# A graph layer with routed experts: ScalarE compares tile numbers behind every fourth slot, 16-bit tables

## The chip, the cores and the metric

The kernel runs on one core of one Trainium2 chip. A core has five engines with queues of their own: PE (TensorE, the matmuls), DVE (VectorE), ACT (ScalarE), POOL (GpSimd) and SP (SyncE, which here only issues DMAs). They run side by side and meet through semaphores. The metric is the device time of one execution in microseconds; what is given is the median of some runs.

## What is computed

There are 3125 nodes with 256 features and 50,000 edges, sorted by destination. The destinations are drawn so that low nodes have most edges.

```python
def gnn(x, W1, b1, W2, b2, src, tgt):            # x is layer-normed
    feat = concat([x[tgt], x[src] - x[tgt]])
    h = relu(feat @ W1 + b1)                     # W1 512x512
    msg = h @ W2 + b2                            # W2 512x256
    out = segment_sum(msg, tgt)
    return out / (degree(tgt) + 1e-8)
def ffn(x):                                      # x is layer-normed
    logits = xn @ Wr + br                        # 8 experts, the best 2, softmax weights
    return sum over both: w * (gelu(xn @ W1[e] + b1[e]) @ W2[e] + b2[e])
x = x + gnn(layernorm(x), ...)
x = x + ffn(layernorm(x))
```

## The kernel before

The nodes lie in 25 tiles of 128 rows. An edge's hidden row is relu(p[dst] + q[src]), with q = x @ W1[lower half] + b1 and p = x @ (upper half less lower half). The sum over a tile's edges is taken before W2. The work has four stages with a barrier of all engines between them.

**Stage A (0 to 66 us).** Tile by tile the rows are normalised, turned, and multiplied to q, which goes to memory (q_rows). VectorE has in between the small work of the tables: from counts it finds where each tile's edges begin (`find_ends`, start_f), how many slots of 128 edges each has (last_f, nslot), the slot's first edge (`find_tiles`, `find_blocks`) and the tile of each slot (ttab). `unsorted` is a flag: where it is set, for edges out of order or tiles that come too soon, `n_pass` becomes 25 instead of 1 and the edges are gone over 25 times. That is the general path. With the reference's inputs the flag is 0. tile4_i holds the tile of each slot as integers, and DMAs copy it to tile_row (on one partition) and to tile_of_slot.

**Stage B, the edge loop (66 to 596 us).** It goes over 408 slots, written out one by one; a few steps called "half" between them make p for later tiles. For a slot j:
- POOL gathers its 128 rows of q into one of 16 places of gath (`fetch`, L1001). It may do so once the place was read, 16 slots back.
- ScalarE copies these rows into one of 5 PSUM banks (`seed`, L1231), or, for one slot in eight, VectorE adds them (`add_z`, L1063).
- PE adds p of the destination: a matmul with a one-hot matrix ohT, high and low part (`expand`, L1381 to L1385).
- ScalarE takes the relu into h_hi (`relu_hi`, L1250), VectorE the rest into h_lo (`split_lo`, L1068).
- PE sums the edges by destination into agg_ps (`sum_edges`, L1428 and L1429). agg_ps has two halves, used in turn by even and odd tiles.
- ScalarE closes the tile when the next slot has another one (`close`, L1252): it waits until PE has summed the slot, compares two registers with the tile numbers of this slot and the next, and if they differ copies the half out (L1260), fills it with zeroes (L1267) and waits for each. Otherwise it jumps over this.

Each engine's order is written out by its own function `first` with a lead: at a step ScalarE does the relu of 5 steps ahead, then the seed of 8 steps ahead, then the close of the slot itself. The relu of a slot waits for the sum four slots back (HI_RING). ScalarE loads the tile numbers of 17 slots into registers at every 16th slot (`load_tiles`, L952), PE four at every fourth.

**Stage C (596 to 685 us)** multiplies by W2, adds, normalises and sorts the tokens by expert. **Stage D (685 to 903 us)** goes over 56 expert slots: gather, two products, and a scatter with addition by POOL, whose waits come from a table turn_i.

## Time and profile before

| what | value |
|---|---|
| median of 3 runs | 1121.46 us (1121.32, 1121.46, 1126.88) |
| span of the profiled execution | 902.9 us |
| around the span, to the median | 218.6 us |
| PE, DVE, ACT, POOL busy | 834.7, 651.0, 628.3, 602.4 us |
| granted TensorE clock, mean | 0.995 |

The page gives the span from the first to the last instruction of the profiled execution, and no other time of it; the time of a run is longer. Register, branch, semaphore and DMA-issuing instructions are not counted as busy. A busy PE is not PE at its peak, since matmuls overlap.

### The profile page before, as it was taken

To read this page: it belongs to the slowest core of one execution; us is meant where nothing else is said; L and a number is where in the kernel's file an instruction comes from. 1 tells how busy PE (TensorE), PEld (TensorE's weight loads), DVE (VectorE), ACT (ScalarE), POOL (GpSimd) and SP (SyncE) were. 2 spreads that over 40 slices of the span, in tenths; PEclk is the share of its full clock that TensorE was granted. 3 is DMA by queue.
4 is the path that set the end of the run, shared out by engine and by line. 5 is a ranking of instruction groups with operands and counts; after the bars stand their busy time and mean duration, and the time that the engine had idled before them with its cause. 6 is when DMAs were issued, how large, how long until landed. Compare 5 with 4: busy or idle time off the path is not lost. (4 is left out here: it accounts for less than half of the span.)

```text
span 902.9 us, 17755 instructions
## 1 busy us (share of the span) xinstructions
PE 834.7 (92%) x4088; PEld 652.2 (72%) x4089; DVE 651.0 (72%) x1764; ACT 628.3 (70%) x1393; POOL 602.4 (67%) x615
## 2 busy tenths in 40 slices
PE   6997999999999989989999999989999999999997
PEld 3444767767676666766666666768888999999996
DVE  6846888888888888878888887756894455455443
ACT  4425788888888888888898889845554555555553
POOL 2317777777777777777777777659404677776764
PEclk9998999999999999999999999999999999999999
DMA  8547777878888778888887878819852344444443
GB/s 255 171 150 220 247 239 245 247 234 251 240 243 236 247 231 243 241 238 238 245 248 235 230 233 264 228 49 281 265 139 54 59 73 75 81 71 68 76 71 45
DMA packets 91000, 169.47 MB, mean 188 GB/s; under 512 B 17604, under 2 KB 56910, under 8 KB 90840
## 3 DMA queue, kind: packets, MB, share of 16 engines
q0 software_dynamic: 43696, 122.35, 49.8%
q1 hardware_dynamic: 46232, 44.79, 17.0%
q10 hardware_dynamic: 944, 0.92, 0.4%
q8 instruction: 44, 0.72, 0.3%
q14 instruction: 84, 0.69, 0.3%
HBM read 146.98 MB, written 21.43 MB: 187 GB/s over the span
## 5 line engine op out<-in xcount | busy, mean ns | idle before, releaser
L1001 POOL DMA_INDIRECT gath<-q_rows,idx_t x408 | 391.9, 960 | 138.8 <-issue 93.3
L1068 DVE SCALAR_TENSOR_TENSOR h_lo<-bank,h_hi 128x512 fp32r<-128x512 f32 x327 | 219.4, 682 | 40.1 <-ACT h_hi L1250 38.0
L1250 ACT ACTIVATE h_hi<-bank 128x512 fp32r<-128x512 f32 x327 | 191.0, 598 | 45.5 <-DVE bank L1063 20.9
L1231 ACT ACTIVATE bank<-gath 128x512 f32<-128x512 f32 x287 | 173.4, 604 | 14.3 <-DMA gath<-q_rows,idx_t 10.5
L1384 PE MATMUL bank<-p_hi,ohT 128*128 x287 | 123.4, 430 | 42.8 <-ACT bank L1231 40.3
L1428 PE MATMUL agg_ps<-h_hi,oh 128*128 128x512 f32 x408 | 161.9, 397 | 0.3 <-DVE h_lo L1068 0.2
L1429 PE MATMUL agg_ps<-h_lo,oh 128*128 128x512 f32 x408 | 161.3, 395 | 0.0
L1995 POOL DMA_INDIRECT out<-y_out,sca_i x56 | 93.7, 1673 | 49.0 <-issue 15.9
L1384 PEld LDWEIGHTS bank<-p_hi,ohT 128*128 128x128 f32 x287 | 54.1, 189 | 91.2 <-issue 83.0
L1385 PE MATMUL bank<-p_lo,ohT 128*128 x287 | 113.9, 397 | 0.0
L2099 PE MATMUL bank<-tokT,fw_now 128*128 128x128 f32 x896 | 109.3, 275 | 0.8 <-ACT tokT L2055 0.8
L2065 ACT ACTIVATE actT<-bank,b1T 128x128 f32<-128x128 f32 x224 | 64.0, 367 | 61.8 <-PE bank L2099 61.8
L2111 PE MATMUL agg_ps<-fw,actT 128*128 x448 | 105.9, 380 | 0.1
L2099 PEld LDWEIGHTS bank<-tokT,fw_now 128*128 128x128 f32 x896 | 104.5, 192 | 1.0 <-DVE fw_now L2018 1.0
L1428 PEld LDWEIGHTS agg_ps<-h_hi,oh 128*128 128x128 f32 x408 | 76.8, 188 | 27.4 <-issue 2.1
L1577 POOL DMA_INDIRECT agg_all<-xm_rows,gat_i x56 | 57.9, 1034 | 57.9 <-DVEq L1817 40.6
L1046 DVE TENSOR_SCALAR oh<-iota_row,rel_t 128x128 fp32r<-128x128 f32 x408 | 91.7, 296 | 4.7 <-issue 4.7
L2038 DVE TENSOR_TENSOR y_out<-agg_ps,b2f 128x256 f32<-128x256 f32 x56 | 23.8, 424 | 95.6 <-PE agg_ps L2111 87.6
L2111 PEld LDWEIGHTS agg_ps<-fw,actT 128*128 128x128 f32 x448 | 80.9, 190 | 9.0 <-issue 0.3
L1429 PEld LDWEIGHTS agg_ps<-h_lo,oh 128*128 128x128 f32 x408 | 76.9, 188 | 11.9
L1056 DVE TENSOR_SCALAR ohT<-rows_sb,slot_no 128x512 fp32r<-128x512 bf16 x102 | 52.1, 512 | 33.7 <-PE bank L1385 26.6
L2055 ACT ACTIVATE tokT<-bank,gain_T 128x128 f32<-128x128 f32 x112 | 45.0, 453 | 38.9 <-PE bank L2089 38.2
(287 smaller groups left out, 1276.6 us busy)
## 6 DMA issues: line engine op xcount, KB each, us to landing
rows_sb<-rel_blocks SPq DMA_DIRECT2D x102, 128.0 KB, 4.3
fw<-in_L_ffn_W SPq DMA_DIRECT2D x16, 512.0 KB, 5.1
gath<-q_rows,idx_t POOLq DMA_INDIRECT x408, 4.4
q_rows<-q_buf SPq DMA_DIRECT2D x25, 256.0 KB, 2.4
out<-x_all SPq DMA_DIRECT2D x28, 128.0 KB, 3.8
x_all<-in_x SPq DMA_DIRECT2D x25, 128.0 KB, 2.7
xm_rows<-xt SPq DMA_DIRECT2D x25, 128.0 KB, 3.0
x_all<-in_x SPq DMA_DIRECT2D x2, 640.0 KB, 10.3
```

The costliest lines, as they stand in the source:

```text
L1001: pool.indirect_dma_start(out=gath[:, j % RING, :], out_offset=None, in_=q_rows[:, :], in_offset=bass.IndirectOffsetOnAxis(ap=idx_t[:, j:j ...
L1046: ins = dve.tensor_scalar(oh[:, q % 4, k, :], iota_row[:], rel_t[:, bass.ds(local + k, 1)], None, ALU.is_equal)
L1068: dve.scalar_tensor_tensor(out=h_lo[:, j % LO_RING, :], in0=z_of(slot0, j), scalar=0.0, in1=h_hi[:, j % HI_RING, :].bitcast(F32), op0=ALU. ...
L1231: actv.activation(z_of(slot0, j), gath[:, j % RING, :], ACT.Copy).then_inc(s_seed, 1)
L1250: actv.activation(h_hi[:, j % HI_RING, :], z_of(slot0, j), ACT.Relu).then_inc(s_hi, 1)
L1384: pe.matmul(z, w, p_hi[:, tile, :], start=False, stop=True, skip_group_check=True)
L1385: pe.matmul(z, w, p_lo[:, tile, :], start=False, stop=True, skip_group_check=True).then_inc(s_exp_seeded, 1)
L1428: pe.matmul(agg_ps[:, par, :], w, h_hi[:, j % HI_RING, :], **more)
L1429: pe.matmul(agg_ps[:, par, :], w, h_lo[:, j % LO_RING, :], **more).then_inc(s_sum, 1)
L1995: pool.indirect_dma_start(out=out[:, :], out_offset=bass.IndirectOffsetOnAxis(ap=sca_i[:, i:i + 1], axis=0), in_=y_out[:, i % OUTS, :], in ...
L2099: ins = pe.matmul(bank[i % 2][:, h * P:(h + 1) * P], fw1_now[:, i % 2, k, h * P:(h + 1) * P], tokT[:, i % 2, k * P:(k + 1) * P], start=(k ...
L2111: ins = pe.matmul(agg_ps[:, i % 2, 0:D], actT[:, i % 2, k * P:(k + 1) * P], fw2[:, experts[i], k, :], start=(k == 0), stop=(k == KH - 1))
```

## The change

- `close_group` takes the place of the call of `close` in the first pass. It calls `close` only behind slots whose number leaves 3 when divided by 4, and behind the last two. Behind a group of four, the tile number of its first slot is compared with that of the slot after its last, instead of a slot's with the next one's.
- A group can hold only one tile end if each tile has at least four slots. `find_ends` therefore gets three instructions that set `unsorted` where a tile from 1 to 23 has fewer, so that the kernel takes the general path, which closes behind each slot as before.
- tile_row, tile4_i, tile_of_slot, group_tile and turn_i have 16-bit numbers instead of 32-bit ones.

```diff
+U16 = mybir.dt.uint16
...
-        tile_row = sb("tile_row", [1, SC * P], I32, edge_ctx)
+        tile_row = sb("tile_row", [1, SC * P], U16, edge_ctx)
...
-        tile4_i = sb("tile4_i", [SC, P], I32, b_ctx)
+        tile4_i = sb("tile4_i", [SC, P], U16, b_ctx)
...
-        turn_i = sb("turn_i", [P, 2, MS], I32)
+        turn_i = sb("turn_i", [P, 2, MS], U16)
...
                     then(dve.tensor_scalar(nslot[:, 1:NT + 1], last_f[:, 0:NT], 1.0, None, ALU.max))
+                    then(dve.tensor_scalar(too_short[:, 2:NT], last_f[:, 1:NT - 1], float(GROUP), None, ALU.is_lt))
+                    now()
+                    then(dve.tensor_reduce(shortest[:, :], too_short[:, 2:NT], AX.X, ALU.max))
+                    now()
+                    then(dve.tensor_tensor(unsorted[:], unsorted[:], shortest[:, :], ALU.max))
                     now()
...
-                def close(slot0, j, vals, last=False):
+                def close_group(j, vals):
+
+                    if j == NS - 1:
+                        close(j - j % UNROLL, j % UNROLL, vals, last=True)
+                    elif j % GROUP == GROUP - 1 or j == NS - 2:
+                        close(j - j % UNROLL, j % UNROLL, vals, first=j // GROUP * GROUP % UNROLL)
+
+                def close(slot0, j, vals, last=False, first=None):
...
-                    cur, nxt = vals[j], vals[j + 1]
+                    cur, nxt = vals[j if first is None else first], vals[j + 1]
...
-                        close(j - j % UNROLL, j % UNROLL, vals, last=j == NS - 1)
+                        close_group(j, vals)
```

The order of the instructions shows what moves. First ScalarE near the end of the edge loop, before: the seed of slot 406 (s_g6), the compare of slot 398 and the body that closes it, the relu of 404, the seed of 407 (s_g7) and the next compare.

```order
L1231 ACTIVATE bank<-gath 128x512 [waits s_g6,s_lo]
L1258 COMPARE_AND_BRANCH [waits s_sum]
L1260 ISA
L1260 REGISTER_ALU
L1260 ACTIVATE agg_all<-agg_ps 128x512
L1265 ISA
L1267 ACTIVATE agg_ps<-zero_r 128x512 [waits s_evac]
L1269 REGISTER_ALU
L1258 UNCONDITIONAL_BRANCH [waits s_evac]
L1250 ACTIVATE h_hi<-deg_ps 128x512 [waits s_sum,s_z]
L1231 ACTIVATE bank<-gath 128x512 [waits s_g7,s_lo]
L1258 COMPARE_AND_BRANCH [waits s_sum]
```

The same place of the changed kernel, whose line numbers are higher (seed L1239, relu L1258, compare L1273):

```order
L1239 ACTIVATE bank<-gath 128x512 [waits s_g6,s_lo]
L1258 ACTIVATE h_hi<-deg_ps 128x512 [waits s_sum,s_z]
L1239 ACTIVATE bank<-gath 128x512 [waits s_g7,s_lo]
L1273 COMPARE_AND_BRANCH [waits s_sum]
L1275 ISA
L1275 REGISTER_ALU
L1275 ACTIVATE agg_all<-agg_ps 128x512
L1280 ISA
L1282 ACTIVATE agg_ps<-zero_r 128x512 [waits s_evac]
L1284 REGISTER_ALU
L1273 UNCONDITIONAL_BRANCH [waits s_evac]
L960 TENSOR_LOAD tile_row [waits s_tiles3]
```

The body now stands behind the relu of 404 and the seed of 407, directly ahead of the load of the next tile numbers. In all, ScalarE's program has 2858 rows instead of 5298; the rows of the five engines' other programs stay, but for VectorE's three.

Second VectorE in stage A, before: the last steps of `find_ends` (last_i, last_f, nslot), the q_buf add of tile 7, and the first of the running sums.

```order
L576 TENSOR_SCALAR last_i<-last_i 128x25 [waits s_dveA]
L578 CAST last_f<-last_i 128x25 [waits s_dveA]
L580 TENSOR_SCALAR nslot<-last_f 128x25 [waits s_dveA]
L528 TENSOR_TENSOR q_buf<-bank,b1g 128x512 [waits s_qst3,s_q_ps,s_dveA]
L588 COPY cumA<-nslot 128x1
```

And of the changed kernel:

```order
L579 TENSOR_SCALAR last_i<-last_i 128x25 [waits s_dveA]
L581 CAST last_f<-last_i 128x25 [waits s_dveA]
L583 TENSOR_SCALAR nslot<-last_f 128x25 [waits s_dveA]
L584 TENSOR_SCALAR too_short<-last_f 128x23
L586 TENSOR_REDUCE shortest<-too_short 128x1 [waits s_dveA]
L588 TENSOR_TENSOR unsorted<-unsorted,shortest 128x1 [waits s_dveA]
L531 TENSOR_TENSOR q_buf<-bank,b1g 128x512 [waits s_qst3,s_q_ps,s_dveA]
L596 COPY cumA<-nslot 128x1
```

Three instructions stand between nslot and the q_buf add; two of them wait for the one ahead.

## Rows read from the trace of the kernel before

**Rows 1.** The page, part 1: busy us (share of the span) and instructions.

```profile
PE 834.7 (92%) x4088; PEld 652.2 (72%) x4089; DVE 651.0 (72%) x1764; ACT 628.3 (70%) x1393; POOL 602.4 (67%) x615
```

**Rows 2.** Groups by line, the gathers: count, busy us, mean ns, idle before, releasers.

```profile
L1001 POOL DMA_INDIRECT gath<-q_rows,idx_t x408 | 391.9, 960 | 138.8 <-issue 93.3 <-ACT bank L1231 21.0 <-POOLq L389 14.7
```

**Rows 3.** The gathers' line by itself: time from issue to landing.

```profile
DMA to landing us min/median/max: 3.4/4.4/7.2
```

**Rows 4.** Waits from 66 to 595 us: us in total, times, longest us.

```profile
POOL gath L1001 <- issue: 93.3, 306, 0.3
...
PE bank L1384 <- ACT bank L1231: 40.3, 54, 4.1
...
POOL gath L1001 <- ACT bank L1231: 21.0, 69, 0.3
ACT h_hi L1250 <- DVE bank L1063: 20.9, 29, 1.4
...
ACT h_hi L1250 <- issue: 6.9, 17, 0.8
```

**Rows 5.** Timeline of POOL, first and last gather: start us, us, instruction, idle before.

```profile
66.33 0.97 POOL L1001 DMA_INDIRECT gath<-q_rows,idx_t  x1 [14.70 <-POOLq L389]
...
581.10 1.18 POOL L1001 DMA_INDIRECT gath<-q_rows,idx_t  x1 [0.30 <-issue]
```

**Rows 6.** Timeline of the edge loop's end, ScalarE and VectorE.

```profile
586.72 0.60 ACT L1231 ACTIVATE bank<-gath 128x512 f32<-128x512 f32 x1
...
587.06 0.69 DVE L1063 TENSOR_TENSOR deg_ps<-deg_ps,gath 128x512 f32<-128x512 f32 x1
...
587.24 0.59 ACT L1260 ACTIVATE agg_all<-agg_ps  x1
...
587.95 0.60 ACT L1267 ACTIVATE agg_ps<-zero_r 128x512 f32 x1
...
588.72 0.60 ACT L1250 ACTIVATE h_hi<-deg_ps 128x512 fp32r<-128x512 f32 x1 [0.18 <-ACT agg_ps L1267]
589.22 0.60 ACT L1231 ACTIVATE bank<-gath 128x512 f32<-128x512 f32 x1
...
590.36 1.62 ACT L1250 ACTIVATE h_hi<-bank 128x512 fp32r<-128x512 f32 x3 [0.54 <-issue]
...
595.66 0.19 DVE L1629 COPY deg<-deg_ps 128x25 f32<-128x25 f32 x1 [2.79 <-PEq L962]
```

**Rows 7.** Windows, 200 us of stage D: busy us (and count) of each engine.

```profile
690.00:890.00 200.00, 199.92 (x1395) 186.21 (x1394) 99.70 (x266) 104.97 (x324) 140.26 (x104) 1.00 0.44 70
```

**Rows 8.** Timeline of ScalarE in the edge loop, relus and seeds in a row.

```profile
568.71 0.60 ACT L1250 ACTIVATE h_hi<-bank 128x512 fp32r<-128x512 f32 x1 [0.31 <-PE deg_ps L1385]
569.21 0.59 ACT L1250 ACTIVATE h_hi<-deg_ps 128x512 fp32r<-128x512 f32 x1
...
580.09 0.61 ACT L1231 ACTIVATE bank<-gath 128x512 f32<-128x512 f32 x1
580.61 0.61 ACT L1250 ACTIVATE h_hi<-bank 128x512 fp32r<-128x512 f32 x1
581.09 0.62 ACT L1231 ACTIVATE bank<-gath 128x512 f32<-128x512 f32 x1
```

**Rows 9.** Timelines of stage A: VectorE's find_ends, ScalarE's root and PE's turn.

```profile
28.70 0.18 DVE L578 CAST last_f<-last_i 128x25 f32<-128x25 int32 x1
28.91 0.18 DVE L580 TENSOR_SCALAR nslot<-last_f 128x25 f32<-128x25 f32 x1
29.12 0.69 DVE L528 TENSOR_TENSOR q_buf<-bank,b1g 128x512 f32<-128x512 f32 x1
...
38.79 0.30 ACT L710 ACTIVATE std<-mv,eps_col 128x5 f32<-128x5 f32 x1 [2.97 <-DVE mv L513]
...
39.63 0.44 PE L757 MATMUL bank<-ident,xn_buf 128*128 128x128 f32 x2 [0.57 <-ACT xn_buf L720]
```

More of the change, by code:

```diff
@@ L118, in build @@
     dst_blocks = nc.dram_tensor("dst_blocks", (EB + 1, P), I32, kind="Internal").ap()
-    tile_of_slot = nc.dram_tensor("tile_of_slot", (SC, P), I32, kind="Internal").ap()
+    tile_of_slot = nc.dram_tensor("tile_of_slot", (SC, P), U16, kind="Internal").ap()
     rel_blocks = nc.dram_tensor("rel_blocks", (SC * P, P), BF16, kind="Internal").ap()
@@ L199, in build @@
         soonest = whole("soonest", [P, 1], F32, a_ctx)
+        too_short = whole("too_short", [P, 32], F32, a_ctx)
+        shortest = whole("shortest", [P, 1], F32, a_ctx)
         dense_i = whole("dense_i", [P, 2, EC], I32, a_ctx)
@@ L241, in build @@
         tile_hot = sb("tile_hot", [P, 2 * NT + 2], F32R, b_ctx)
-        tile4_i = sb("tile4_i", [SC, P], I32, b_ctx)
+        tile4_i = sb("tile4_i", [SC, P], U16, b_ctx)
         group_hot = sb("group_hot", [P, 2 * NG], F32R, b_ctx)
-        group_tile = sb("group_tile", [NG, GROUP], I32, b_ctx)
+        group_tile = sb("group_tile", [NG, GROUP], U16, b_ctx)
         tile_f = sb("tile_f", [NG, GROUP], F32, b_ctx)
```

## The prediction

> **What bounds the kernel now.** I first read the shares of busy time, then who waited for whom in the edge loop, and only then single stretches. The shares point the wrong way: PE is busy 92% and POOL 67% [rows 1]. But each of POOL's 408 gathers takes 0.95 us and is followed by 0.30 us in which POOL issues the next, which no busy share counts. The group of the gathers has 391.9 us busy and 138.8 us idle before them, 14.7 of it ahead of the first; 516.0 us are left for 408 gathers, 1.265 us each [rows 2]. The view of waits says the same from the other side: of the gathers' waits none is longer than 0.3 us, whoever is named as the releaser, and where ScalarE is named (69 times) the gap is no longer than where nobody is [rows 4]. So POOL never waits for a ring place. The first gather starts at 66.33 us, the last at 581.10 us [rows 5]: 514.8 us for 407 steps, again 1.265. Nothing in the diff touches POOL's stream in this loop. That fixes the place of the last gather relative to the first, whatever ScalarE does.
>
> What ScalarE can change is how far behind the gathers the rest runs. A gather's rows land 4.4 us (median) after its issue [rows 3]. The seed of slot 407, ScalarE's copy of the last gathered rows into PSUM, starts at 589.22 us, 8.1 us after that gather began [rows 5, 6]. So 8.1 - 4.4 = 3.7 us at the loop's end are backlog of the other engines. This is all that a quicker ScalarE can win in this loop. Behind the loop stand the stages from 595.66 us on [rows 6], which the change leaves alone but for one table of POOL's; in a 200 us stretch there PE is busy 199.92 us [rows 7], so POOL's table is not in the path.
>
> **The comparisons taken out.** Before, each of 408 slots ends with one wait, one compare and a jump over eight instructions; 24 tile ends and the last slot really close. After, 102 slots compare (one in four; the last group compares twice, 103 in all). 305 compares go. What is one worth? Two relus with a compare between them and no seed (568.71 and 569.21) stand 0.50 us apart, and relu to seed with no compare between (580.61 to 581.09) 0.48; seed to relu with a compare is 0.52 (580.09 to 580.61) [rows 8]. The step is set by what ran before, and the compare costs 0.00 to 0.04 us of ScalarE's time, since the sequencer does it while the previous tile is still being worked on. I take 0. At 0.04 the 305 would be 12 us of ScalarE's time, more than the whole backlog, and the gain would stop at the 3.7 us above.
>
> The Trainium skill ("Advanced Engine Details and Errata", Control Flow Timing) prices a compare-and-branch at about 108 ns and an unconditional branch at about 51 ns. By that price 305 compares would be some 33 us of sequencer time, an estimate from that page; the spacing of at most 0.04 us in [rows 8] says that nearly all of it lies beside running instructions. By either price the loop would end at most 3.7 us sooner.
>
> The wait that goes with each compare was never the last one: at the same step the relu ahead of it waits for the sum of a later slot (HI_RING is 4 and it runs 5 ahead), so it is already met.
>
> **The closes that move.** The reference's destinations give 81, 33, 26 ... 9, 9, 8, 4 slots a tile. Of the 24 tile ends before the last, 7 close three slots later, 6 two, 7 one, and 4 where they did. The close itself stays: 587.24 to 588.72, 1.48 us of ScalarE [rows 6]. Who waits for it? PE needs that half of agg_ps two tiles on. The shortest tile between has 8 slots; a close 3 slots later leaves 5 slots, 6.3 us, less the slot or two by which ScalarE runs behind. No new wait of PE.
>
> The one that counts is the last, slot 398, in the drain. Now it runs before the relu of slot 404 and the seed of 407; then it runs behind them. Step by step [rows 6]: the seed of 406 starts at 586.72 as before. The relu of 404 needs VectorE's add, which ends at 587.75, so it starts near 587.92; the seed of 407 at 588.42 (0.50 later), 0.80 us sooner than now. The close follows: copy 588.94, zeroes 589.65, end and return as before 0.77 us later, 590.42. But now the load of the next 17 tile numbers stands right behind it, ahead of the relu of 405. That load today makes relu 405 start 1.14 us behind the seed instead of 0.50, so it costs up to 0.64. Relu 405 starts between 590.42 and 591.06 instead of 590.36. The last three relus, splits and sums follow it at ScalarE's pace. The loop's end moves by +0.1 to +0.7 us; I take the middle, +0.4.
>
> **The three instructions on VectorE.** The test for short tiles stands in the early stage, between nslot (28.91) and the q_buf add (29.12). Chained small instructions there stand 0.21 us apart [rows 9]; the first of the three needs no wait, about 0.1, the other two 0.21 each: +0.5 us. Does something hide it? VectorE has no idle time there, and the next hop is in the rows: the root at 38.79 waited 2.97 us for VectorE's mv, and PE then sat idle 0.57 us for xn_buf at 39.63 [rows 9]. An idle PE hides nothing, and behind it PE runs without a pause for VectorE, so the 0.5 us reaches the first gather: 66.33 becomes 66.8. Ends: 0 if a gap takes it, 0.63 (3 x 0.21). I take 0.5.
>
> **The 16-bit tables.** The number of loads stays, on ScalarE (26 in the loop), PE and POOL. How long one takes no row shows apart from the 0.64 us above and 17 idle times of 6.9 us in sum before relus [rows 4]. If a 16-bit load costs nothing, the drain is 0.64 us shorter, if twice as much, 0.64 longer; the 25 others, and PE's, stand where POOL's 1.265 a slot hides them: PE sat idle 40.3 us there for ScalarE's seeds [rows 4], and a later start of PE's shows first in that idle time. I take 0, as nothing shows a load's cost to hang on its bytes.
>
> **Sum.** +0.5 early, 0 for the compares, +0.4 in the drain, 0 for the tables: +0.9 us. The span of 902.9 becomes 903.8. The page gives no time of its own for this execution besides the span; the median of the runs is 1121.46, 218.6 more, and I leave those 218.6 as they are: 903.8 + 218.6 = 1122.4. I say 1122.3.
>
> **Rivals.** (A) The compares do cost ScalarE time and the backlog goes. For it: PE waited 40.3 us for ScalarE's seeds in this loop, 54 times [rows 4]. Against: [rows 8]. Price: -3.7 at the end, the closing order then hardly matters, +0.5 early: 1118.3. Still within 0.5%.
>
> (B) Slower: a moved close falls upon a tight spot, the relu of an added slot, where ScalarE already waited 20.9 us for VectorE [rows 4]. Then every close adds to the backlog instead of being absorbed. With g us for each of 24 closes the end comes 24g later, gathers or not; at 0.35 us this is +8.4, with +0.9 from the sum: 1130.8. It decides from g = 0.2 (4.8 + 0.9 = 5.7). Against it: closes fall on all four positions already and the backlog stays at some 8 us.
>
> (C) The 218.6 us around the span hang on the program. ScalarE's program shrinks from 5298 rows to 2858, the whole by 18%. Were all of it proportional, -40 us: 1082; a tenth of that is -4, 1118. Nothing in the trace speaks for it. The Trainium skill ("Runtime: NRT & Kernel Launch", The launch sequence) puts what NRT adds around a kernel at some 9 to 15 us; the 218.6 us here are far more, so the page does not explain them either.
>
> (D) The change doesn't do its work: a tile counted as short would send the kernel through 25 passes, over ten milliseconds. The test covers tiles 1 to 23, whose smallest has 8 slots; the tile with 4 is the last and left out, and it would not be under four either. I give it nothing.
>
> **Chances.** Forecast 0.66, A 0.18, B 0.09, C 0.07. What this measurement can tell from no change is about 0.5%, 5.6 us. Faster by more: most of C, and a little of A, 0.10. Slower by more: most of B, 0.08. Within: 0.82. The forecast's own range is 1120 to 1124. The range for 8 in 10 reaches down past A to 1117 and up to 1126.5, near where B begins to count and where one of the three runs of before lay.
>
> **What will show it.** First gather near 66.8, last 514.8 us later, longest idle before a gather still 0.3; else the bound was misread. Nslot to q_buf 0.7 instead of 0.21. The seed of 407 some 7 to 7.5 us behind its gather, followed by the close. If it starts at 4.4, A holds; if the lag grows past 10, B. If the span keeps and the time moves, C.

## The result, and the profile after

The changed kernel takes 1112.6 us (median of four runs, 1107.8 to 1113.4), the kernel before, timed beside it, 1122.4 (1121.3 to 1126.9). The ratio is 0.988, with a 95% interval from 0.984 to 0.992. The ratio is an estimate of its own from all the runs; the two medians by themselves divide to 0.991, inside that interval. In a later group of runs on one chip it was 0.984 (0.981 to 0.987). So the change makes the kernel 1.2 to 1.6% faster by the two ratios, and 0.8 to 1.9% by their intervals. The prediction was 1122.3 and no change.

The first thing to read in the profile after is not a row but a difference. The profiled run of the changed kernel took 1112.8 us, and its span is 1110.7:

```profile
core 0: 1110.7 us, clock 0.916
```

```profile
PE 908.7 (82%) x4088; PEld 700.3 (63%) x4089; DVE 651.4 (59%) x1767; ACT 627.5 (56%) x1393; POOL 600.3 (54%) x615
```

Nothing of any size lies around this span. The 218.6 us that stood "around" the span of before are therefore not overhead. The busy times of DVE, ACT and POOL are those of [rows 1] to within 2.1 us, and PE's grew by 74.0, and yet the span is 208 us longer. Where they are lost shows in the gathers' group and in who waited for whom from 66 to 800 us (total, times, longest):

```profile
L1009 POOL DMA_INDIRECT gath<-q_rows,idx_t x408 | 389.4, 954 | 327.4 <-DVE bank L1071 139.1 <-issue 102.6 <-DVE deg_ps L1071 36.4
```

```profile
PEld bank L1399 <- issue: 192.4, 130, 8.2
DVE h_lo L1076 <- issue: 145.1, 84, 5.0
POOL gath L1009 <- DVE bank L1071: 139.1, 38, 5.0
PE bank L1399 <- ACT bank L1239: 112.7, 49, 7.5
...
ACT h_hi L1258 <- remote: 74.2, 28, 6.9
```

In [rows 2] POOL had 138.8 us of idle time before gathers, and in [rows 4] none of those gaps was over 0.3 us. Here POOL waits 38 times for up to 5.0 us for VectorE's add into bank, and 10 times more for one into deg_ps, of a slot 16 earlier: the ring of 16 is full, and POOL no longer sets the pace. The first gather starts at 66.65 us and the last at 767.93, 1.72 us apart on average, where [rows 5] give 1.265.

What the edge loop does in this form repeats every 8 slots. POOL:

```profile
334.35 0.95 POOL L1009 DMA_INDIRECT gath<-q_rows,idx_t  x1 [4.68 <-DVE bank L1071]
335.60 0.95 POOL L1009 DMA_INDIRECT gath<-q_rows,idx_t  x1 [0.30 <-issue]
...
343.12 0.94 POOL L1009 DMA_INDIRECT gath<-q_rows,idx_t  x1 [0.30 <-issue]
348.09 0.95 POOL L1009 DMA_INDIRECT gath<-q_rows,idx_t  x1 [4.03 <-DVE bank L1071]
```

PE, and then ScalarE, over the end of that burst of 8 gathers:

```profile
342.66 0.40 PE L1400 MATMUL bank<-p_lo,ohT 128*128 x1
342.90 0.39 PE L1381 MATMUL deg_ps<-oh,group_hot 128*102 128x512 f32 x1
343.13 0.39 PE L1443 MATMUL agg_ps<-h_hi,oh 128*128 128x512 f32 x1
343.36 0.40 PE L1444 MATMUL agg_ps<-h_lo,oh 128*128 128x512 f32 x1
347.23 0.49 PE L1399 MATMUL bank<-p_hi,ohT 128*128 x1 [3.47 <-ACT bank L1239]
```

```profile
341.49 0.60 ACT L1239 ACTIVATE bank<-gath 128x512 f32<-128x512 f32 x1
344.38 0.60 ACT L1258 ACTIVATE h_hi<-deg_ps 128x512 fp32r<-128x512 f32 x1 [2.30 <-PE bank L1400]
345.89 0.60 ACT L1258 ACTIVATE h_hi<-bank 128x512 fp32r<-128x512 f32 x1 [0.92 <-remote]
346.39 0.60 ACT L1239 ACTIVATE bank<-gath 128x512 f32<-128x512 f32 x1
```

PE's last matmul begins at 343.36 us. Its increments arrive far later. These are the recorded arrivals of semaphore increments from PE in the same stretch, which the page does not show:

```
344.36 expand   345.81 sum   345.85 expand   345.90 sum   345.94 expand(added)
345.98 expand   346.02 count   346.06 sum
```

The last seven arrive within 0.25 us of each other. In kind and order they match the seven matmuls that increment and begin from 340.71 to 343.36 us, so the first comes 4.7 us behind its matmul's end and the last 2.3. (The ends of matmuls are modelled; whether the increments travel late or the matmuls end late the trace doesn't say.) ScalarE's relus wait for them, its seeds come after the relus in its queue, and PE then stands 3.47 us for a seed. I call this a stand. In the changed kernel PE has 58 gaps over 1 us in the loop, 165 us in all; 23 lie at slots 0 mod 16 and 18 at slots 8 mod 16. In the trace of before there were 6 such gaps, 10.5 us in all. PE's clock falls with them. The same 200 us of the loop before, and then after:

```profile
300.00:500.00 200.00, 180.94 (x743) 133.52 (x742) 167.24 (x401) 174.00 (x338) 151.81 (x158) 1.00 0.81 240
```

```profile
300.00:500.00 200.00, 152.91 (x548) 111.33 (x546) 120.71 (x291) 123.45 (x242) 108.35 (x114) 0.89 0.62 175
```

A matmul takes 0.28 us of PE's busy time there instead of 0.24, at a granted clock of 0.89 instead of 1.00. In the clock records of the trace it goes between its two levels, 2.4 and 1.2 GHz: from 100 to 810 us it falls 32 times, 31 of them within 1.6 us of the end of such a gap, and stays low for 157 us. That goes with PE's 74.0 us of added busy time, and the gaps are the other part of what the loop lost. I call the loop with stands the slow form and that of the shown trace of before the fast form.

One caution: the trace after does not hold all increments. It has 306 for the 408 sums, and 9,591 updates of semaphores in all, where the trace of before has all 408 and 17,107. Every trace of the slow form below lacks as many (8,626 to 11,914 updates are there), and none of the fast form does (17,043 or more). So a match by kind and order may be wrong, and so may a releaser that a row names. But the relus at 344.38 and 345.89 start 0.02 and 0.04 us behind arrivals in the list.

Behind the loop nothing changed: PE is busy all of the time in stage D, as in [rows 7], and 150 us hold about as many matmuls as before (1044, against 1395 in 200 us).

```profile
900.00:1050.00 150.00, 150.00 (x1044) 139.71 (x1044) 75.84 (x200) 79.06 (x244) 106.28 (x78) 1.00 0.44 70
```

One term of the sum can be read at once, stage A, where [rows 9] had 28.91 and 29.12:

```profile
28.74 0.18 DVE L583 TENSOR_SCALAR nslot<-last_f 128x25 f32<-128x25 f32 x1
28.83 0.17 DVE L584 TENSOR_SCALAR too_short<-last_f 128x23 f32<-128x23 f32 x1
29.03 0.18 DVE L586 TENSOR_REDUCE shortest<-too_short 128x1 f32<-128x23 f32 x1
29.25 0.16 DVE L588 TENSOR_TENSOR unsorted<-unsorted,shortest 128x1 f32<-128x1 f32 x1
29.44 0.69 DVE L531 TENSOR_TENSOR q_buf<-bank,b1g 128x512 f32<-128x512 f32 x1
```

Nslot to q_buf is 0.70 us instead of 0.21, as predicted, and the first gather starts 0.3 us later (66.65 against 66.33).

The loads of table values into registers are in the trace too, though the page does not count them. Their durations in the loop, before and after:

```
                                    32 bits (before)     16 bits (after)
ScalarE, 17 values, x26             1.24 to 1.27 us      3.57 to 3.63 us
GpSimd, 8 values, x14 (stage D)     0.56 to 0.86 us      1.81 to 2.15 us
TensorE, mostly 4 values, x102      1.00 us (median)     0.99 us (median)
```

The tables of half the width made the load on ScalarE three times as long, 0.21 us a value in place of 0.07. The Trainium skill ("Runtime: NRT & Kernel Launch", Instruction fetch mechanics) puts a load into registers, which its page knows as one from HBM, at about 200 ns per register, even in bulk. These loads read an SBUF table; the 16-bit ones come out at that figure, the 32-bit ones at a third of it. Read with this, the gain of 1.2% is a riddle: the only part of the change with a visible cost is a loss, and the whole is faster.

### The profile page after: what moved, and what is told of

It is laid out like the page before. It is cut to its first block and busy times, and to the rows that moved or that the text cites. A ratio compares the mean times of both kernels' runs of the same rounds, so it can differ in the third digit from the quotient of the medians.

```text
span 1110.7 us, 17453 instructions
## 1 busy us (share of the span) xinstructions
PE 908.7 (82%) x4088; PEld 700.3 (63%) x4089; DVE 651.4 (59%) x1767; ACT 627.5 (56%) x1393; POOL 600.3 (54%) x615
## 5 line engine op out<-in xcount | busy, mean ns | idle before, releaser
L1258 ACT ACTIVATE h_hi<-bank 128x512 fp32r<-128x512 f32 x327 | 191.7, 598 | 208.7 <-remote 61.8
L1399 PE MATMUL bank<-p_hi,ohT 128*128 x287 | 140.5, 489 | 144.0 <-ACT bank L1239 112.7
L1399 PEld LDWEIGHTS bank<-p_hi,ohT 128*128 128x128 f32 x287 | 61.9, 216 | 201.6 <-issue 192.4
L1443 PE MATMUL agg_ps<-h_hi,oh 128*128 128x512 f32 x408 | 180.2, 442 | 5.9 <-DVE h_lo L1076 4.7
L1444 PE MATMUL agg_ps<-h_lo,oh 128*128 128x512 f32 x408 | 178.4, 437 | 0.0
L1239 ACT ACTIVATE bank<-gath 128x512 f32<-128x512 f32 x287 | 173.8, 606 | 8.0 <-DMA gath<-q_rows,idx_t 4.8
L1400 PE MATMUL bank<-p_lo,ohT 128*128 x287 | 128.2, 447 | 0.0
L1443 PEld LDWEIGHTS agg_ps<-h_hi,oh 128*128 128x128 f32 x408 | 88.1, 216 | 35.2 <-issue 7.1
L1444 PEld LDWEIGHTS agg_ps<-h_lo,oh 128*128 128x128 f32 x408 | 88.2, 216 | 17.5
L1054 DVE TENSOR_SCALAR oh<-iota_row,rel_t 128x128 fp32r<-128x128 f32 x408 | 88.9, 294 | 8.1 <-issue 4.4
L1064 DVE TENSOR_SCALAR ohT<-rows_sb,slot_no 128x512 fp32r<-128x512 bf16 x102 | 49.3, 484 | 57.3 <-remote 33.8
L1076 DVE SCALAR_TENSOR_TENSOR h_lo<-deg_ps,h_hi 128x512 fp32r<-128x512 f32 x81 | 55.6, 687 | 43.5 <-issue 37.0
```

The costliest lines, as they stand in the source:

```text
L1054: ins = dve.tensor_scalar(oh[:, q % 4, k, :], iota_row[:], rel_t[:, bass.ds(local + k, 1)], None, ALU.is_equal)
L1076: dve.scalar_tensor_tensor(out=h_lo[:, j % LO_RING, :], in0=z_of(slot0, j), scalar=0.0, in1=h_hi[:, j % HI_RING, :].bitcast(F32), op0=ALU. ...
L1239: actv.activation(z_of(slot0, j), gath[:, j % RING, :], ACT.Copy).then_inc(s_seed, 1)
L1258: actv.activation(h_hi[:, j % HI_RING, :], z_of(slot0, j), ACT.Relu).then_inc(s_hi, 1)
L1399: pe.matmul(z, w, p_hi[:, tile, :], start=False, stop=True, skip_group_check=True)
L1400: pe.matmul(z, w, p_lo[:, tile, :], start=False, stop=True, skip_group_check=True).then_inc(s_exp_seeded, 1)
```

## The experiments

Two questions had to be told apart: where the timed runs of before spend 218 us that its trace does not have, and which part of the change gains. Each group below ran on one chip, with the kernel before timed between. By the record's numbers the chips of the six groups are 2, 2, 13, 5, 8 and 11. So the first two groups carry the same number, although the kernel before took 1124.5 us in one and 1107.2 in the other, 25 minutes later; the record does not say whether it is the same piece of hardware.

A note that holds for all kernels with 32-bit tables here. They carry a mask of bits on the tile number ahead of each wait that is computed from it (`& 127`), which changes no value. It adds one register instruction per slot on TensorE, and its cost is the ratio of the first run.

### First group: what part gains

**again32**, before with the masks:

```diff
-   pe.wait_ge(s_evac, tile * 2 + (CREDIT - 2))
+   pe.wait_ge(s_evac, (tile & 127) * 2 + (CREDIT - 2))
+   cur = actv.snap(cur & 127)        # in a close, ahead of its waits
-   pool.wait_ge(s_put[...], turn[back - 1][i])
+   pool.wait_ge(s_put[...], turn[back - 1][i] & 2047)
```

> The kernel before, with one bit mask more in the fused register operation ahead of each sum on TensorE, in each close on ScalarE and in each wait on a finished row in stage D (none changes a value). It is there for its trace. Theory S: the timed executions of the kernel before run the edge loop at about 1.7 us per slot, as the changed kernel's do (701.2 us from its first to its last gather), and not at the 1.265 us of the trace of before; then this run has a span within 5 us of its time, some 1119 us, and gathers 1.70 to 1.76 us apart. Rival F: the edge loop runs at 1.265 us per slot in every execution and some 219 us lie around the span; then the span is 903 and the time 1122.

Measured: 1128.8 us, ratio 1.0027 (1.0008 to 1.0046), span 1125.5, gathers 1.78 us apart. Theory S holds: this is the loop of before as it is timed, and it is the slow form.

```profile
core 0: 1125.5 us, clock 0.902
```

```profile
L1001 POOL DMA_INDIRECT gath<-q_rows,idx_t x408 | 387.8, 951 | 352.6 <-DVE bank L1063 163.8 <-issue 110.0 <-DVE deg_ps L1063 41.8
```

**after_i32**, the changed kernel with 32-bit tables:

```diff
-U16 = mybir.dt.uint16
+U16 = mybir.dt.int32        # and the masks
```

> The changed kernel with its tables back at 32 bits (with the same masks as the run above). In the two traces ScalarE's load of 17 table values took 1.25 us at 32 bits (26 loads) and 3.6 us at 16. Theory L: in the loop's slow form this load is not covered, so the change to 16 bits cost 26 x 2.35 = 61 us or, where half is covered, 30, and this kernel takes 1050 to 1085. Rival C: all is hidden, or the slow form has another cause, and this kernel takes 1112 as the changed one does.

Measured: 1127.2, ratio 1.0019 (0.9999 to 1.0039). Both theories missed. Theory L wanted a large gain from shorter loads; in fact the whole gain of the change is gone. Against again32 (1.0027) the closes behind every fourth slot are worth 0.1%, inside both intervals.

**before_u16**, before with 16 bits in the five places of the diff and nothing else:

```diff
-   tile_row = sb("tile_row", [1, SC * P], I32, edge_ctx)
+   tile_row = sb("tile_row", [1, SC * P], U16, edge_ctx)    # and tile_of_slot, tile4_i, group_tile, turn_i
```

> The kernel before with 16-bit tables and nothing else. Theory L: 30 to 61 us longer than before, 1150 to 1183. Rival C: 1122. Rival T (the tables, not the closes, bring what the change won): 1113.

Measured: 1113.7, ratio 0.989 (0.986 to 0.992). Rival T, to which I had given least thought, is right: the 16-bit tables bring the gain, the closes next to nothing.

**after_dummy**, a compare that never holds in every slot without a close:

```diff
+   else:
+       never(j - j % UNROLL, j % UNROLL, vals)   # If(cur > nxt): a close's body
```

> The changed kernel, and in each slot that has no close a compare that is never true, around a body like that of a close. Theory K (the 305 compares and their taken jumps over a body are what the change saved): this gives it back, 1122 or more. Rival M (that closes stand behind every fourth slot saved it, whatever the compares cost): 1112.

Measured: 1115.9, ratio 0.990 (0.987 to 0.994), against 0.988 of the change. With 305 compares given back the two intervals overlap by most of their width, so Theory K falls, and the prediction's 0 for the compares stands in the slow form too. (Rival M had the closes' places as the gain; after_i32 and before_u16 speak against that.)

### Second group: which load

The kernel before took 1107.2 us in this group, so only ratios compare.

**act16** and **pe16**: before with the masks, and one engine alone reads 16 bits.

```diff
+   tile_low = tile_row[:].bitcast(uint16).rearrange("o (s two) -> o s two", two=2)
-   tile_row[0:1, bass.ds(at, n)]
+   tile_low[0:1, bass.ds(at, n), 0] if engine == ... else tile_row[0:1, bass.ds(at, n)]
```

> The kernel before with the masks of the first run, where ScalarE alone reads the low halves of the 32-bit tile table as 16-bit values; TensorE and GpSimd read 32 bits. Theory A: the gain of the 16-bit tables (11 us in the run before_u16) comes from ScalarE's longer load (3.6 us in place of 1.25): 1128.8 - 15 = 1114, with slot 8 of each 16 at 3.1 us in place of 3.8. Rival P (it comes from TensorE's own loads): 1129 or more, and slots 8k as in again32.

> The same with TensorE alone reading 16-bit values. Theory P: 1114, and TensorE's rows of 0.7 us ahead of slots 8k go, as in before_u16 (7 of them against 67 in again32). Theory A: 1129.

Measured: act16 0.991 (0.989 to 0.994), pe16 1.004 (1.002 to 1.006). Against again32's 1.003, ScalarE's load of 3.6 us alone gives 1.1%, and TensorE's gives nothing. Theory A.

**after_turn32**, the changed kernel with GpSimd's table of stage D back at 32 bits:

```diff
-   turn_i = sb("turn_i", [P, 2, MS], U16)
+   turn_i = sb("turn_i", [P, 2, MS], I32)                   # and its mask
```

> The changed kernel with GpSimd's table of stage D alone back at 32 bits. The edge loop of again32 ends 15.3 us behind that of before_u16, the span only 11.8, so 3.5 us are given back in stages C and D; GpSimd's 14 loads there take 1.9 us in place of 0.57. Theory G: these loads give it back, so 1112.5 - 3 = 1109. Rival: the stages' own scatter, 1112.5.

Measured: 0.9895 (0.986 to 0.993), against 0.988 with the 16-bit table. Theory G wanted 0.3% less, which is no more than the half-width of either interval, so the ratio alone does not decide it. The traces do: from the last sum to the end it is 312.9 us here and 312.6 with the 16-bit table. GpSimd's loads, 1.3 us longer each, are hidden in stage D, and the 3.5 us given back behind the loop are not theirs.

**lead8**, after_turn32 with gathers held to 8 slots ahead:

```diff
-   wait_after(pool, s_seed, seeded + seeded_before(j - RING))
+   wait_after(pool, s_seed, seeded + seeded_before(j - LEAD))   # LEAD = 8; s_z alike
```

> The run above with gathers no more than 8 slots ahead of their use (16 before). In the slow loop gathers come in bursts of 8, and TensorE stands until the burst's transfers end; in the trace of before no gather was more than 6 slots ahead. Theory B (the long lead makes the bursts, and they make the stand): the loop comes nearer to 1.27 us per slot, 1000 or less. Rival N (the stand is TensorE's own, the lead only its mirror): 1109 within 10 us, or longer by what a gather then arrives late.

Measured: 1084.3, ratio 0.979 (0.975 to 0.983). Rival N: the steps from slot to slot are those of after_turn32 (15.1 and 12.1 us for the two halves of 16 slots, against 15.4 and 11.8), and the stands stay. But there are 10 us less before slot 16, where the first and longest stand is, so it is 1% faster than its parent. Its ratio is the lowest of all runs, though its interval overlaps that of act_three below.

### Third group: another chip, another loop

**act32x3** (two more loads of 17 values, not used), **act_8** (three more of 9 values at each eighth slot, not used), **pe_more** and **quarter**:

```diff
+   for _ in range(2): load_tiles(mybir.EngineType.Activation, local0, UNROLL + 1)   # act32x3
+   for _ in range(3): load_tiles(mybir.EngineType.Activation, j, 9)                 # act_8
+   for _ in range(5): settle(pe)                    # pe_more, ahead of each sum
-   out=gath[:, j % RING, :], in_=q_rows[:, :]
+   out=gath[:, j % RING, 0:H // 4], in_=q_rows.rearrange("r (a h) -> (r a) h", a=4)[:, :]   # quarter
```

> The kernel before with the masks of the first run (again32, ratio 1.0027), where ScalarE loads its 17 table values of 32 bits three times in a row, 3.75 us per 16 slots in place of 1.25 (at 16 bits one load took 3.6 us, and the loop got shorter). Theory W (any wait of ScalarE there does it, the width is beside the point): ratio 0.991, as act16. Rival V (it is the 16-bit form of the load): 1.003 or, with 26 x 2.5 us more on ScalarE, up to 1.06.

> The same as again32, with three loads of 9 values more on ScalarE at every eighth slot (some 2 us each time). Theory W, if one wait per 16 slots gains 13 us, two gain as much or up to twice that: 0.98 to 0.99. Rival V: 1.003 or more.

> again32 with five semaphore increments more per slot on TensorE (0.05 us each where nothing holds it back). TensorE stands at slots 8k, and from one stand to the next it goes through about 127 instructions of its queue. Theory I (the stand hangs on the instructions gone through): the stands come every 6 slots or so and no longer at 8k, and the loop grows by a third of its stands, some 50 us, ratio 1.04 to 1.05. Rival S (it hangs on the slots, by what is done at every eighth): they stay at 8k, ratio 1.003 to 1.01.

> again32 with gathers of a quarter of each row (64 KB in place of 256), used four times over; the sums are of other values. Theory D (the stands and the rows of 0.7 us on TensorE come from the gathers' transfers): no row of 0.7 us, the loop 1.27 us per slot by GpSimd's 408 gathers, 900 to 910. Rival N (they don't): 1110 or more.

Here the kernel before took 903.8 us (22 runs). That is the form of the trace from which I predicted, span 902.9. act32x3 1.002, act_8 1.0035 and quarter 1.000 tell nothing apart: the chip has no slow form, and the unused loads of the first two were not in the program (their traces have 26 loads on ScalarE), so these two are again32 once more. This is what the group does show: again32's code, which took 1128.8 us in the first group, takes 905.4 here. The program does not set the form of the loop. The chip, or what state it is in, does.

```profile
core 0: 905.7 us, clock 0.997
```

```profile
L1001 POOL DMA_INDIRECT gath<-q_rows,idx_t x408 | 390.9, 958 | 138.9 <-issue 96.9 <-ACT bank L1231 21.6 <-POOLq L389 14.9
```

pe_more took 1114.1, ratio 1.235 (1.232 to 1.238), and missed both its theories. Its trace has the five increments 0.151 us apart, not 0.05, in every slot: 0.75 us more on TensorE's sequencer, and steps of 1.51 us in most slots. It has one gap over 1 us. TensorE became the bound; that is no stand. But POOL, with the ring full, goes through bursts of 8 gathers and waits here as well, 46 of them over 3 us from gather to gather, all ahead of slots 4 mod 8:

```profile
308.90 0.95 POOL L1001 DMA_INDIRECT gath<-q_rows,idx_t  x1 [4.48 <-DVE deg_ps L1063]
...
317.78 0.95 POOL L1001 DMA_INDIRECT gath<-q_rows,idx_t  x1 [0.30 <-issue]
323.09 0.94 POOL L1001 DMA_INDIRECT gath<-q_rows,idx_t  x1 [4.36 <-DVE bank L1063]
```

So such a burst is what a full ring looks like, and on this chip it brings no stand.

### Fourth group: a wait, and the bytes

The kernel before took 1125.7 us. **after_again** is the changed kernel unaltered, **act_three** has three loads of 17 values at 32 bits, all used, and quarter_b is the kernel quarter.

```diff
-   return load_tiles(mybir.EngineType.Activation, local0, UNROLL + 1)
+   sets = [load_tiles(mybir.EngineType.Activation, local0, UNROLL + 1) for _ in range(3)]
+   return [sets[n % 3][n] for n in range(UNROLL + 1)]
```

> The changed kernel as it is. The kernel before took 1121 to 1124 us on one chip, 1107 on another and 904 on the one of the last call, where it ran the edge loop at 1.27 us per slot. Theory R (there are two forms of the loop, and it is the chip that sets which): if this chip runs before at 904, the change is worth what the prediction's sum says, +0.9 us, ratio 1.000 to 1.003; if it runs before at 1107 or more, 0.988 as measured. Rival Q (the change gains 1% wherever it runs): 0.988 here too.

> again32 with three loads of the 17 table values (32 bits) in a row on ScalarE per 16 slots, all three of them used (in the run act32x3 two were unused and had been left out of the program, so that it was again32 once more). On a chip with the slow loop, theory W (a wait of 3.75 us of ScalarE does it, whatever its form): 0.991. Rival V (only the 16-bit form): 1.003 to 1.06. On a chip with the fast loop: 26 x 2.5 = 65 us more on ScalarE, which has 3.7 us of backlog to give at the end of the loop; it is busy 0.6 of the time there, so 1.003 to 1.02.

> again32 with gathers of 64 KB in place of 256 (the sums are of other values). On a chip with the slow loop, theory D (TensorE's stands come from the gathers' transfers): the loop at 1.27 us per slot, 900 to 910. Rival N: 1100 or more. On a chip with the fast loop nothing is told apart: 903.

Measured: after_again 0.984 (0.981 to 0.987), as the change before. It fell on a chip with the slow form, so Theory R was not put to the test. act_three 0.982 (0.979 to 0.984): Theory W. A wait of 3.75 us on ScalarE, made of 32-bit loads, gains 2.1% against again32, whose ratio comes from another group. The 16-bit form of the table has no merit of its own; it made ScalarE stop for longer. quarter_b 1.0015 (0.999 to 1.004), gathers 1.79 us apart: with a quarter of the bytes the stands are all there, so Theory D falls. POOL in quarter_b goes through the same burst and wait as at 334.35 above:

```profile
284.43 0.95 POOL L1001 DMA_INDIRECT gath<-q_rows,idx_t  x1 [4.88 <-DVE bank L1064]
285.69 0.95 POOL L1001 DMA_INDIRECT gath<-q_rows,idx_t  x1 [0.31 <-issue]
```

### Fifth and sixth group: count, second wait, pace

**pe_two**, two increments per slot as in pe_more, and **act_each8**, six used loads of 9 values at every eighth slot in place of one of 17 at every sixteenth:

```diff
+   settle(pe); settle(pe)                           # pe_two, ahead of each sum
+   if j % 8 == 0:
+       sets = [load_tiles(mybir.EngineType.Activation, j, 9) for _ in range(6)]
+       now8[:] = [None] * (j % UNROLL) + [sets[n % 6][n] for n in range(9)]
```

> again32 with two semaphore increments more per slot on TensorE (0.15 us each in the run pe_more, where five of them made TensorE the bound on a chip with the fast loop). On a chip with the slow loop, theory I (TensorE's rows of 0.7 us come after a fixed number of its instructions, some 127 by the trace of again32): the stands leave slots 8k and spread over all slots mod 16, one every 7 slots. Rival S (they belong to every eighth slot): they stay at 8k and 16k; the loop grows by less than 408 x 0.3. On a chip with the fast loop TensorE has 0.3 us a slot to give: 1.003 to 1.03.

> again32 with six loads of 9 table values (32 bits, all used) in a row on ScalarE at every eighth slot, 3.5 us each time, in place of one load of 17 per sixteenth. act_three, 3.75 us once per 16 slots, gave 0.982. On a chip with the slow loop, theory W2 (each stand is shortened by a wait of ScalarE ahead of it, at 8k as at 16k): 0.96 to 0.97. Rival H (one wait per 16 slots moves the stands apart and that is all it can do; the second costs its own time): 0.982 to 1.01. On a chip with the fast loop: 51 x 3.5 - 33 = 145 us more on an engine that is busy 0.6 of 515 us: 1.003 to 1.10.

The kernel before took 1107.8 us. pe_two 1.028 (1.025 to 1.032): with an eighth more instructions on TensorE between them (142 rows of the trace per 8 slots in place of 126), the stands still come every 8 slots, now mostly at slots 7 and 15 mod 16 (25 of 37 gaps over 1 us), and POOL still waits 5.2 us ahead of each eighth gather. Rival S. act_each8 1.023 (1.019 to 1.027): no second gain, Rival H, and worse than its 1.01. Its stands left slots 0 and 8 and stood at 4 and 12 mod 16. What is remarkable is what it did not cost: ScalarE's loads took 237 us in place of 33, and the loop ran at 1.81 us per slot, where again32 had 1.82 in the first group.

**paced**, lead8 with two increments ahead of each gather on GpSimd, and the added slots' gathers held by the ring of 16 alone:

```diff
-   wait_after(pool, s_z, added + added_before(j - LEAD))
+   wait_after(pool, s_z, added + added_before(j - RING))
+   settle(pool); settle(pool)                       # ahead of each gather
```

> The kernel of lead8 (the changed kernel with GpSimd's table at 32 bits and gathers at most 8 slots ahead; ratio 0.979 on a chip with the slow loop), with two semaphore increments ahead of each gather on GpSimd, and gathers for the slots that VectorE adds held back by the ring of 16 alone, so that GpSimd goes at a steadier and slower pace. In every slow trace GpSimd sends 8 gathers 1.25 us apart, then waits 4 to 5 us, and TensorE's rows of 0.7 us stand at the end of such a burst. Theory E (the burst on GpSimd brings the stand): with 1.25 + 2 x 0.1 us per gather there are none, the loop takes some 408 x 1.45 = 592 us, and the kernel about 980. Rival M (the burst is only how the ring fills behind a stand that comes by itself): 1080 to 1110, ratio 0.97 to 0.99, with stands at 8k. On a chip with the fast loop: 408 x 0.2 = 82 us more, some 985, ratio 1.09.

Before took 902.9 us: a chip with the fast form, so Theory E was not tested. Measured: 959.7, ratio 1.062 (1.060 to 1.064); gathers 1.39 us apart on average in place of 1.265, which is 50.6 us of the 56.9. But the run did not pace GpSimd at all. The two increments take 0.017 us each, 0.08 us apart, while the gather ahead of them still runs, and 349 of the 407 steps from gather to gather are under 1.30 us. So it could not have tested Theory E on a chip with the slow form either. What made the loop longer is another thing, here at slot 176:

```profile
305.52 0.95 POOL L1010 DMA_INDIRECT gath<-q_rows,idx_t  x1 [0.30 <-issue]
308.23 0.97 POOL L1010 DMA_INDIRECT gath<-q_rows,idx_t  x1 [1.77 <-ACT bank L1242]
309.50 0.95 POOL L1010 DMA_INDIRECT gath<-q_rows,idx_t  x1 [0.30 <-issue]
```

```profile
302.19 0.60 ACT L1242 ACTIVATE bank<-gath 128x512 f32<-128x512 f32 x1
305.48 1.09 ACT L1261 ACTIVATE h_hi<-bank 128x512 fp32r<-128x512 f32 x2 [2.69 <-issue]
306.45 0.61 ACT L1242 ACTIVATE bank<-gath 128x512 f32<-128x512 f32 x1
```

In the 2.69 us ScalarE does its 16-bit load of 3.59 us (301.79 to 305.38), the seeds come behind it, and POOL, at most 8 slots ahead, waits for one of them. Of the 50.6 us, 40.1 are in the steps to the gathers of slots 0 mod 16. PE then has 36 gaps over 1 us, 58 us in all, 23 of them at slot 4 mod 16. So the longer load, which gains in the slow form, costs some 40 us, 4%, in the fast one when gathers are at most 8 slots ahead. How much of this a lead of 16 would hide was not run.

### What the groups say together

Steps from slot to slot of TensorE's sums, summed over the first and the second 8 slots of each 16 (means over slots 32 to 384, us):

```
                    first 8   second 8     ratio
before (fast form)    10.10      10.07     (the shown trace)
again32               14.77      14.05     1.003
before_u16            15.47      12.45     0.989
after                 15.36      12.59     0.988
act_three             15.31      12.51     0.982
pe16 (2nd group)      14.09      13.83     1.004
act16 (2nd group)     15.46      11.95     0.991
```

ScalarE's longer load stands at slot 0 of each 16. It makes the first half 0.5 to 0.7 us longer, and the second half 1.5 to 1.6 us shorter in the runs whose kernel before took 1122 to 1126 us: the stand at slot 8 shrinks (3.8 us for that step in again32, 3.1 in before_u16, 2.5 in act_three), and so does the step into the next slot 0 (2.5, 1.9 and 2.3 us). This is the gain. In before_u16 it is 15.3 us at the last slot's sum.

## Why the prediction was wrong

**What bounds the kernel now** is the step that failed. It read the trace well: 408 gathers at 1.265 us, no wait over 0.3, 3.7 us of backlog. But it took that trace for the execution that is timed, in which POOL waits up to 5.0 us and its gathers are 1.72 us apart. Its own sign of a misread bound, a longest idle time over 0.3 us before a gather, has come true. "The median of the runs is 1121.46, 218.6 more, and I leave those 218.6 as they are": those 218.6 us were the difference of two forms of the same loop. again32 shows it on one side (time 1128.8, span 1125.5) and the 903.8 us of the third group on the other. The prediction had a rival for the 218.6 (C), which hung them on the program's size. It was wrong too: after_i32 has the shorter program of the change and gains nothing. The hint was in the numbers. The profiled run of the changed kernel has 2.1 us around its span; I had written myself that 218.6 were left unexplained, and that was the moment to doubt that the trace and the times belong together.

**The 16-bit tables** were the term with the wrong price in the form that is timed. I took 0, "as nothing shows a load's cost to hang on its bytes", with ends of 0.64 us. ScalarE's load went from 1.25 to 3.6 us, 26 times; the loads' own rows lay in the trace of before, and I had looked for them only in the gaps between counted instructions. The sign of the effect I could not have had from them. In the slow form 2.3 us more on ScalarE once per 16 slots made the loop 15 us shorter.

**The comparisons taken out**, 0: right in the slow form (after_dummy, after_i32). **The closes that move**: 0.1% at most. The drain itself was another one: slot 407's seed stands 20.6 us behind its gather (788.54 and 767.93), not 7 to 7.5, as the ring was full. Behind it the order is the predicted one, the close right behind the seed:

```profile
788.54 0.60 ACT L1239 ACTIVATE bank<-gath 128x512 f32<-128x512 f32 x1
789.06 0.59 ACT L1275 ACTIVATE agg_all<-agg_ps  x1
789.77 0.60 ACT L1282 ACTIVATE agg_ps<-zero_r 128x512 f32 x1
794.16 1.57 ACT L1258 ACTIVATE h_hi<-bank 128x512 fp32r<-128x512 f32 x3 [3.79 <-issue]
```

The load of the next tile numbers stands in the 3.79 us before the relus. So the end of the 16-bit term, "if twice as much, 0.64 longer", was an edge too near: the load became 2.9 times as long. **The three instructions on VectorE**, 0.5: right, 0.49 measured, 0.3 at the first gather.

**The rivals.** A and B were both about the backlog behind POOL, which does not bind in the slow form. None of the rivals had a loop in which POOL waits for the others, because [rows 4] exclude it for their execution. The measured 1112.6 lies between A's 1118.3 and C's 1082, but the mechanism of neither made it: the compares cost nothing and the program's length gains nothing. With a measured spread of 5 us around 1121 and a trace of 903, a rival "the timed loop is not this loop" deserved a good part of the chance, and a range far wider than 1117 to 1126.5.

**What stays open.** Not shown: why PE's increments arrive late and in bursts, and why a wait of ScalarE shortens the next stand and not its own. The runs exclude the gathers' bytes (quarter_b), the compares and the program's length (after_dummy, after_i32), and a fixed number of PE's instructions between two stands: the stands come every 8 slots with 118 rows of PE in the trace per 8 slots (after), with 126 (again32) and with 142 (pe_two). In every slow trace POOL waits ahead of most gathers of a slot that VectorE adds (slots 4 mod 8) and mostly goes through the 8 from there in one burst. It does so in pe_more too, on a chip with the fast form and without stands, so there the burst is only how a full ring looks. Whether the burst has a part in the stands of the slow form no run has told: paced did not remove it, and its chip had no stands. Two rivals were not tested. The period of VectorE's adds is 8 slots too, and no run changed it. And the record has a span and a granted clock for every timed run, so each was recorded in some way; since the slow traces are those that lack records, the recording itself may have a part, and no run was timed without it. The change itself was never timed on a chip with the fast form. The prediction's sum of +0.9 us was made for that form and is neither confirmed nor refuted; paced, which holds the change, is 56.9 us slower than before there, with gathers at most 8 slots ahead.

## What to carry to other kernels

Before a profile is used, compare the span of the profiled execution with the times: if they differ by more than a few us (2.1 here), the trace shows another execution than the one that is to be sped up, and the bound read from it may not be the bound. Narrow tables are not cheaper to load into registers; look up the loads' own rows. In a loop that runs in lockstep through a full ring, a wait added to one engine can come out as a gain, so a part that gains should be tried in another shape (here three 32-bit loads) before its reason is believed. Such a gain belongs to the form of the loop that it was measured in: the same load holds POOL up in paced. And an experiment's own trace shows whether its edit did what it was meant to; the gathers of paced kept their 1.25 us.

## What the runs showed of the hardware

- Two forms of one program. The kernel before took 1124.5, 1107.2, 903.8, 1125.7, 1107.8 and 902.9 us (medians) in the six groups, and within a group its runs spread by 10 us at most. No chip number of the record shows both forms. The granted clock, as the mean of an execution, was 0.90 to 0.94 in the slow form and 0.99 to 1.00 in the fast one (0.98 to 0.99 in paced); pe_more, as long as the slow ones, had 0.991, so a loop of this length does not by itself lower the clock.
- A load of 17 table values into ScalarE's registers takes 1.25 us at 32 bits and 3.6 us at 16; 8 values on GpSimd 0.57 and 1.9; 9 values at 32 bits on ScalarE 0.77. Four values on TensorE take 1.0 us at either width.
- All traces of the slow form lack records of semaphore updates: 8,626 to 11,914 are there, against 17,043 to 19,149 in the fast form. In the loop it is 4,732 (after) against 11,324 (before).
- TensorE's semaphore increments by themselves come 0.151 us apart, though each row shows 0.051.
- In the slow form with the masks, many of TensorE's register instructions at the end of a burst take 0.70 us each in place of 0.04 to 0.09: 101 rows of 0.66 to 0.74 us in again32. The shown trace of before and every other trace of the fast form have none, before_u16 and after, without masks, have 13 and 7, and so few can come with masks too (11 in act_each8). The stands are as long with them as without.
- Gathers of 64 KB are issued in the same 0.95 us as those of 256 KB.
